# A graph kernel on one core: pairwise late statistics in the node stage, the degree roots moved ahead in the opening, and the filter kept in rows of 4 KB

## The reference

```python
deg = segment_sum([edge_weight, 1], [dst, loop]); r = rsqrt(deg)         # one root per node
agg = segment_sum((x @ W)[src_all] * (r[src_all]*w_all*r[dst_all])[:, None], dst_all)
x1  = layernorm(x + relu(agg + b))                                       # layer 1 with its residual
h   = softplus(rbf @ Wf1 + bf1) - log 2;  F = h @ Wf2 + bf2              # the filter, one row an edge
m   = F * (x1[dst] projected by Win_s, Win_v and the edge's direction Y) # messages
S, V = segment_sum(m * edge_weight, src) @ (W1, W2) with a softplus on S
out = layernorm(x1 + [S, V])                                             # layer 2 with its residual
```

## Time and profile before

| | |
|---|---|
| Time, median of 3 runs | 1192.75 us (1190.2 to 1195.69) |
| Profiled execution: its time, its span | 1193.07 us, 1191.3 us |
| Busy share of the span: PE, DVE, ACT, POOL | 84%, 70%, 59%, 55% |
| Mean granted TensorE clock | 0.902 of full speed |
| Moved by DMA | 289 MB, 243 GB/s on average |

### The profile page before, as it was taken

One profiled execution on the slowest core, in us unless ns is written; L12 is line 12 of the kernel. 1 busy time (PEld: TensorE's weight loads), 2 busy tenths in 40 slices (PEclk: granted clock), 3 DMA queues, 4 the chain that ended last, 5 costly groups with the idle time before them and its releaser, 6 DMA issues.

```text
span 1191.3 us, 23227 instructions
## 1 busy us (share of the span) xinstructions
PE 1000.9 (84%) x5088; PEld 790.9 (66%) x5088; DVE 835.9 (70%) x2538; ACT 701.7 (59%) x1632; POOL 660.3 (55%) x812
## 2 busy tenths in 40 slices
PE   7479998998838999999999399999999999634442
PEld 7458777776627888888888267777777777433332
DVE  8578876787606777787777366666666666368887
ACT  0068787777725666666666344444444444268887
POOL 3038888888745777777777546656566664400000
PEclk9999988999878999999999789999999999955555
DMA  9949999999986788878887669999999998589998
GB/s 356 418 156 235 245 228 229 247 253 227 220 170 207 265 276 279 277 277 278 278 277 263 235 161 211 194 202 195 205 194 208 195 205 177 69 256 347 351 351 287
DMA packets 175015, 289.00 MB, mean 243 GB/s; under 512 B 18514, under 2 KB 75750, under 8 KB 174966
## 3 DMA queue, kind: packets, MB, share of 16 engines
q1 hardware_dynamic: 120982, 176.23, 44.2%
q0 software_dynamic: 35840, 83.91, 36.7%
q10 hardware_dynamic: 18144, 28.32, 6.3%
HBM read 139.49 MB, written 148.90 MB: 242 GB/s over the span
## 4 chain that ended last, share of the span: by engine, by line
PE 30%; issue 17%; POOL 11%; DMA 5%; DVE 2%; ACT 2%; POOLq 2%; SPq 1%; ACTq 0%; DVEq 0%
PE bank L1084 6%; PE bank L1095 4%; POOL tiny L463 3%; PE bank L1093 3%; POOL tiny L466 3%; PE bank L1105 3%; PE bank L1107 3%; PE bank L1108 3%; DMA node_mem<-sum 3%; PE bank L1077 2%; PE bank L1085 1%; PE bank L1091 1%; PE bank L1057 1%; POOL tiny L470 1%; POOL tiny L468 1%
## 5 line engine op out<-in xcount | busy, mean ns | idle before, releaser
L500 POOL DMA_INDIRECT sum<-R_mem,l_sidx x80 | 128.0, 1600 | 126.1 <-ACT R_mem L625 74.3
L449 POOL DMA_INDIRECT sum<-R_mem,sidx_all x80 | 133.6, 1670 | 53.1 <-issue 29.1
L1057 PE MATMUL bank<-W0h,G_hi 128*128 128x512 f32 x320 | 134.0, 419 | 1.0 <-ACT G_lo L600 0.9
L1057 PE MATMUL bank<-W0l,G_hi 128*128 128x512 f32 x320 | 126.2, 394 | 0.0
L1057 PE MATMUL bank<-W0h,G_lo 128*128 128x512 f32 x320 | 126.2, 394 | 0.0
L611 ACT ACTIVATE node_mem<-node_mem,tiny 128x512 f32<-128x512 f32 x80 | 65.4, 818 | 91.7 <-POOL tiny L472 91.7
L476 POOL TENSOR_TENSOR G_lo<-node_mem,G_hi 128x512 fp32r<-128x512 f32 x80 | 104.4, 1305 | 17.8 <-ACT G_hi L607 17.8
L880 DVE SCALAR_TENSOR_TENSOR edge_mem<-edge_mem,Y,bank 128x128 f32<-128x128 f32 x240 | 72.5, 389 | 57.4 <-ACT edge_mem L639 57.4
L639 ACT COPY edge_mem<-bank 128x256 f32<-128x256 f32 x80 | 29.9, 373 | 134.3 <-PE bank L1095 134.3
L984 PE MATMUL bank<-G_hi,M_mem 128*128 128x512 f32 x200 | 88.5, 442 | 17.8 <-ACT R_mem L544 17.6
L492 POOL DMA_INDIRECT G_mem<-x_d,dst_i x80 | 79.5, 993 | 35.3 <-issue 23.2
(11 more groups left out here) (172 smaller groups left out, 2953.0 us busy)
## 6 DMA issues: line engine op xcount, KB each, us to landing
sum<-zeros ACTq DMA_DIRECT2D x42, 512.0 KB, 13.7
filt_d<-node_mem SPq DMA_DIRECT2D x40, 512.0 KB, 5.1
node_mem<-sum SPq DMA_DIRECT2D x80, 256.0 KB, 2.8
G_mem<-x SPq DMA_DIRECT2D x80, 256.0 KB, 2.8
x_d<-node_mem SPq DMA_DIRECT2D x80, 256.0 KB, 2.1
node_mem<-filt_d SPq DMA_DIRECT2D x80, 256.0 KB, 4.6
sum<-node_mem SPq DMA_DIRECT2D x80, 192.0 KB, 2.3
out<-G_mem SPq DMA_DIRECT2D x20, 512.0 KB, 4.2
```

The source lines that it names most:

```text
L449: pool.indirect_dma_start(sum0, bass.IndirectOffsetOnAxis(ap=sidx[:, t:t + 1], axis=0), R[t % 8][:, :], None, compute_op=ALU.add).then_inc ...
L500: pool.indirect_dma_start(sum1, bass.IndirectOffsetOnAxis(ap=l1_sidx[:, t:t + 1], axis=0), R3[t % 8][:, :], None, compute_op=ALU.add).then ...
L1057: ins = pe.matmul(bank[4 + a][:, :], zt[b][:, c * P:(c + 1) * P], w[:, c, :], start=(c == 0 and k == 0), stop=(c == 3 and k == 2))
```

## The change

**Node stage 0.** The sum is no longer split before the transposes. PE transposes it as float32 (four transposes), ACT casts the high part out of PSUM (`n_hi`), and DVE subtracts that from the same bank for the low part (`n_lo`). PE multiplies by W0 with the eight matmuls of the high part first. After the bias (`n_pre`), ACT takes the maximum with 0 (`n_rel`), POOL adds x (`n_sum`), and DVE takes statistics two steps later. The inverse root is made for two tiles at once, every second step, and the normalising lies at lag 9 where it lay at 6. The result has eight buffers, where it had four.

**Opening.** ACT issues 8 of the 42 DMAs of zeros and SP the other 34, behind the loads. The roots of the degrees are taken as soon as the degrees are there; Y and the scaled copies of W1 and W2 are made after edge stage 0. In the first two groups the comparisons of indices stand later on DVE, and the first sums earlier on PE and ACT. Gathers of a group share a semaphore.

**Filter.** `filt_d` has a row of 4 KB for two tiles, stored as it lies in its buffer, and is read two tiles at a time, 512 KB.

```diff
     x1_d = nc.dram_tensor("x1_d", (NP, D), F32, kind="Internal").ap()
-    filt_d = nc.dram_tensor("filt_d", (NP, D), F32, kind="Internal").ap()
+    filt_d = nc.dram_tensor("filt_d", (T2 * P, 2 * D), F32, kind="Internal").ap()
...
-        z_hi, z_lo = G_hi[:4], G_lo[:4]
+        zT_hi, zT_lo = G_hi[:4], G_lo[:4]
-        sl, res, W0_s = ([b[:, q * D:(q + 1) * D] for b in node_mem] for q in range(3))
+        sl, W0_s = ([b[:, q * D:(q + 1) * D] for b in node_mem] for q in (0, 2))
+        res = [b[:, q * D:(q + 1) * D] for q in (2, 3) for b in node_mem]
...
-        filt = [b[:, 0:512] for b in node_mem]
+        filt = [b[:, 0:1024] for b in node_mem]
...
+            for s in range(2):
+                sp_.dma_start(fT[s][:, :], rbf[:, s * Q:(s + 1) * Q]).then_inc(w_fT[s], 16)
+            sp_.wait_ge(s_zero, 1)
+            for j in range(NZ, 42):
+                sp_.dma_start(zero_rows(j), zeros[:, :]).then_inc(s_zero0, 16)
+
+
+            for s in range(2, T4 + 3):
                 if s < T4:
-                    if s >= 2:
-                        sp_.wait_ge(w_pre, s - 1)
+                    sp_.wait_ge(w_pre, s - 1)
                     sp_.dma_start(fT[s % 2][:, :], rbf[:, s * Q:(s + 1) * Q]).then_inc(w_fT[s % 2], 16)
                 if s >= 3:
                     for i in (2 * (s - 3), 2 * (s - 3) + 1):
                         sp_.wait_ge(w_eva, 4 * (i + 1))
-                        sp_.dma_start(pair_rows(filt_d, i, 0, D), wst[i % 4]).then_inc(w_st[i % 4], 16)
+                        sp_.dma_start(filt_d[i * P:(i + 1) * P, :], filt[i % 4]).then_inc(w_st[i % 4], 16)
 
...
 
             def nodes0(s, u):
-                a = u % 4
                 if live(s, 0):
-                    held(sp_, n_hi, s - 3)
-                    held(sp_, n_lo, s - 3)
+                    a = u % 4
+                    held(sp_, n_tr, s - 3)
...
-                    held(sp_, n_res, K_RES * (s - 7))
+                    held(sp_, n_sum, s - 7)
                     sp_.dma_start(xl[u], rows(x, s)).then_inc(n_xl[u], 16)
-                if live(s, 8):
-                    t = s - 8
+                if live(s, 12):
+                    t, a = s - 12, (u - 12) % 8
                     held(sp_, n_x1, t + 1)
                     sp_.dma_start(rows(x1_d, t), res[a]).then_inc(n_st[a], 16)
...
+            for g in range(T2):
+                if g >= 4:
+                    sp_.wait_ge(f_M, 2 * (g - 3))
+                sp_.dma_start(trow3[g % 4][:, :], src_row[:, g * 256:(g + 1) * 256].broadcast_to([P, 256])) \
+                   .then_inc(f_trow[g % 4], 16)
+                if g >= 4:
+                    sp_.wait_ge(f_m, 2 * K_PROD * (g - 3))
+                sp_.dma_start(filt[g % 4], filt_d[g * P:(g + 1) * P, :]).then_inc(f_filt[g % 4], 16)
...
-                    .then_inc(e_gather[k], 16)
+                    .then_inc(e_gather[k // 4], 16)
...
+                if live(s, 7) and u % 2 == 0:
...
+                    held(pool, n_mv, t + 2)
+                    st.mark(pool.tensor_scalar(w[:, 0, :], var, EPS, None, ALU.add))
+                    st.mark(pool.tensor_scalar(w[:, 7, :], mean, -1.0, None, ALU.mult))
+                    held(pool, n_rs, 2 * (g + 1))
+                    st.mark(pool.tensor_tensor(w[:, 3, :], w[:, 2, :], w[:, 2, :], ALU.mult))
+                    st.settle(pool)
+                    st.mark(pool.tensor_tensor(w[:, 4, :], w[:, 3, :], w[:, 0, :], ALU.mult))
...
+                    st.mark(pool.tensor_scalar(w[:, 3, :], w[:, 4, :], -0.5, 1.5, ALU.mult, ALU.add))
...
+                    st.mark(pool.tensor_tensor(w[:, 5, :], w[:, 3, :], w[:, 2, :], ALU.mult))
+                    st.settle(pool)
+                    st.mark(pool.tensor_tensor(w[:, 6, :], w[:, 7, :], w[:, 5, :], ALU.mult))
+                if live(s, 4):
+                    t, a = s - 4, (u - 4) % 8
+                    pool.wait_ge(n_rel, t + 1)
+                    pool.tensor_tensor(res[a], res[a], xl[a], ALU.add).then_inc(n_sum, 1)
...
+            for j in range(NZ):
+                act.dma_start(zero_rows(j), zeros[:, :]).then_inc(s_zero0, 16)
...
-                if live(s, 5):
-                    t, a = s - 5, (u - 5) % 4
-                    act.wait_ge(n_res, K_RES * (t + 1))
-                    act.activation(tiny[a][:, 1:2], mv[a][:, 1:2], ACT.Ln, bias=eps_c[:, :]).then_inc(n_rs, 1)
+                tail = live(s, 7) and u % 2 == 0
+                if tail:
+                    t, a = s - 8, u // 2
+                    g = t // 2 if isinstance(t, int) else (t - u) // 2 + a
+                    act.wait_ge(n_mv, t + 2)
+                    act.activation(tiny[a][:, 1, :], mv[a][:, :, 1], ACT.Ln, bias=eps_c[:, :]).then_inc(n_rs, 1)
                 if live(s, 2):
-                    b, t2 = u % 2, s - 2
-                    act.wait_ge(n_tr, s - 1)
-                    wait(act, n_mm, s - 3)
-                    act.copy(zT_hi[b][:, :], bank[b][:, :]).then_inc(n_zT, 1)
-                if live(s, 5):
-                    act.wait_ge(n_rs, 2 * t + 1)
-                    act.activation(tiny[a][:, 2:3], tiny[a][:, 1:2], ACT.Exp, scale=-0.5).then_inc(n_rs, 1)
-                if live(s, 2):
-                    act.copy(zT_lo[b][:, :], bank[2 + b][:, :]).then_inc(n_zT, 1)
+                    t2, b = s - 2, (u - 2) % 4
+                    act.wait_ge(n_tr, t2 + 1)
+                    wait(act, n_mm, t2 - 3)
+                    act.copy(zT_hi[b][:, :], bank[b][:, :]).then_inc(n_hi, 1)
...
+                if tail:
+                    act.wait_ge(n_rs, 2 * g + 1)
+                    act.activation(tiny[a][:, 2, :], tiny[a][:, 1, :], ACT.Exp, scale=-0.5).then_inc(n_rs, 1)
+                if live(s, 4):
+                    t4, c = s - 4, (u - 4) % 8
+                    act.wait_ge(n_pre, t4 + 1)
+                    act.activation(res[c], res[c], ACT.Relu).then_inc(n_rel, 1)
+                if live(s, 9):
+                    t8, c = s - 9, (u - 9) % 8
+                    k, b = c % 2, c // 2
+                    g8 = t8 // 2 if isinstance(t8, int) else (t8 - c) // 2 + b
+                    act.wait_ge(n_rstd, K_ROOT * (g8 + 1))
+                    act.activation(res[c], res[c], ACT.Identity, bias=tiny[b][:, 6, k:k + 1], scale=tiny[b][:, 5, k:k + 1]) \
                        .then_inc(n_x1, 1)
...
-            dve.wait_ge(s_sqrt, 2)
...
+            def inverse_root():
+                dve.wait_ge(s_sqrt, 1)
+
+                link(dve.reciprocal(dis[:, :], degs[:, :]))
+                link(dve.tensor_tensor(degt[:, :], degt[:, :], dis[:, :], ALU.mult))
+                link(dve.tensor_tensor(degt[:, :], degt[:, :], dis[:, :], ALU.mult))
+                link(dve.tensor_scalar(degt[:, :], degt[:, :], -0.5, 1.5, ALU.mult, ALU.add))
+                link(dve.tensor_tensor(dis[:, :], dis[:, :], degt[:, :], ALU.mult))
+                link(dve.tensor_tensor(dis[:, :], dis[:, :], deg[:, :], ALU.mult))
+                dve.sem_inc(s_dis, 1)
...
+                if s == 0:
+                    counts1()
+                    inverse_root()
+                if s >= 2:
+                    counts0()
+                    if s < T4:
+                        counts1()
                 if s >= 1:
                     if g >= 2:
                         dve.wait_ge(e_mm, 4 * (g - 1))
+                    dve.wait_ge(e_trow, g + 1)
...
+                    if s == 1:
+                        counts0()
+                        counts1()
...
+            dve.wait_ge(s_sqrt, 2)
+            link(dve.reciprocal(rn[:, :], rn[:, :]))
+            link(dve.scalar_tensor_tensor(Y[:, :, :], rij[:, :, :], Y1, rn[:, :].unsqueeze(2).broadcast_to([P, T, 3]),
+                                          ALU.mult, ALU.mult))
...
-                if live(s, 4):
                 if live(s, 0):
                     c = u % 4
                     dve.wait_ge(n_sl[c], 16 * (turn(s, c, 4) + 1))
                     dve.wait_ge(n_xl[u], 16 * (turn(s, u, 8) + 1))
                     dve.scalar_tensor_tensor(sl[c], xl[u], dis[:, bass.ds(s, 1)], sl[c], ALU.mult, ALU.add).then_inc(n_z, 1)
+                if live(s, 6):
+                    t, c, a = s - 6, (u - 6) % 4, (u - 6) % 8
+                    dve.wait_ge(n_sum, t + 1)
+                    dve.bn_stats(stat[c][:, :], res[a]).then_inc(n_bn, 1)
+                if live(s, 2):
+                    t, b = s - 2, (u - 2) % 4
+                    dve.wait_ge(n_hi, t + 1)
+                    wait(dve, n_mm, t - 3)
+                    dve.tensor_tensor(zT_lo[b][:, :], bank[b][:, :], zT_hi[b][:, :].bitcast(F32), ALU.subtract).then_inc(n_lo, 1)
+                if live(s, 6):
+                    t, a = s - 6, (u - 6) % 8
+                    k, b = a % 2, a // 2
+                    if k == 0:
+                        held(dve, n_x1, t - 6)
+                    held(dve, n_bn, t + 1)
+                    dve.bn_aggr(mv[b][:, k, :], stat[a % 4][:, :]).then_inc(n_mv, 1)
...
```

(57 more changed lines are left out.)

167 lines of the change are left out of this document (59 added, 108 removed).

## The result

The changed kernel takes 1149.33 us (median of 4 runs, 1146.42 to 1150.51), the kernel before 1192.33 in the same session: a ratio of 0.9633, 95% interval 0.9604 to 0.9662. The forecast was 1160, in a range from 1140 to 1184. The profiled execution took 1146.42, 46.65 less than the one profiled before.

A forecast was written before the change was run, and what follows sets the result against it. It took ACT's queue to delay the opening, DMA to bound edge stage 0, PE node stage 0 and edge stage 1. 1193.07 - 17.5 (opening) - 3 (filter) - 14 (node stage 0) + 1.5 (edge stage 1), less 0.3: 1160 us, range 1140 to 1184.

The forecast's parts named there:

- node stage 0's steps: Node stage 0: a tile every 3.55 us in place of 3.745, giving -15.6 us of the stage's -14.
- the opening: Start to first scatter: from 88.96 to 71.5 us, -17.5, bounds -20 and -13, carried through edge stage 0.
- the filter: Edge stage 0: half as many rows stored could shorten each group where the DMA is full; -3 us, bounds 0 and -10.
- The ready time of 63 to 68: Opening: when the first scatter's sums and indices would be ready, in us, ahead of the zeros' end near 71.5.
- Rival (C): Edge stage 0: swallows the opening's gain, its end doesn't move; 1177 us, chance 0.10.
- the stage is a chain of DMA: Edge stage 0: DMA-paced from the first scatter, share 0.99, a group every 13.29 us, so the whole stage shifts.
- The low ends give 3.44, the high ones 3.85. I take 3.55: Node stage 0: us per step from summing ACT's and DVE's durations and hand-overs around their waits.
- The ring: Node stage 0: a loop of waits between ACT and DVE sets the step at 3.55 us; PE at 3.25 idles.
- Rival (A): Node stage 0: ACT and DVE overlap more, the loop doesn't bind, PE decides at 3.3 us; 1140 us, chance 0.09.
- (B): Node stage 0: the loop over ACT and DVE is long, 3.85 us a tile; 1184 us, chance 0.12.
- (D): Node stage 0: PE loses its full clock, a tile takes 5.5 us; 1316 us, chance 0.04.
- The boundary: Last bias to first gather of edge stage 1: +2 us for the last tile leaving later, +1.5 for larger filter loads.

The follow-up runs named there:

- opening_old: The changed kernel with the opening of before (all 42 DMAs of zeros on ACT's queue, old order of the first groups): 1161.83 us, ratio 0.9762.
- node_alone: The kernel before with only the new node stage 0, opening and filter as before: 1160.09 us, ratio 0.973.
- no_store: The changed kernel with the filter's stores cut to 16 of 128 rows and every load reading the first block: 1151.65 us.
- the memsets: The changed kernel with two or four memsets added on POOL in each group of edge stage 0: 1163.32 us with two, 1174.17 with four.
- ring_broken: The changed kernel with DVE's bias placed ahead of its subtraction in node stage 0: 1139.68 us, ratio 0.9579; repeated, 1141.98 us, ratio 0.9574.
- ring_long: The changed kernel with DVE's scaled sum placed between its subtraction and its bias in node stage 0: 1199.54 us.
- pe_less: The changed kernel without the four matmuls of the low part in node stage 0, the waits kept: 1148.11 us.

## Why the prediction was right

**Right in the whole, one term too small by half.** The time lies in the range, and 10.7 us under the forecast. By the table, node stage 0's steps gave 18.6 more than I took, the opening 2.2 and the filter 2.9 less. So the total is nearer than its largest term, in part because the misses have opposite signs, which is luck.

**The opening: right in size, its last wait in one profile of two ways.** In the profile after, the zeros are late next, as forecast, at 73.7 where I had 71.5. That the last bytes trickle (57 GB/s from 70 to 75) is not in the estimate by bandwidth. The ready time of 63 to 68 was 69. In eight of the ten profiles with this opening it was about 74, behind degrees that came 5 us later, and POOL waited for that: the term is then -13.8 to -14.4, inside the bounds of -20 and -13, and the first group loses 2 to 5 us more. Rival (C), a gain swallowed in edge stage 0, is out as a whole by opening_old; that a part is swallowed, and how much, stays open after node_alone.

**The filter: the reason was wrong.** "Where the DMA is full, this could shorten each group" took the share of 0.99 as the bound, as did "the stage is a chain of DMA". no_store shows that the stage doesn't feel fewer bytes, and the memsets that it feels POOL's queue.

**Node stage 0: the mechanism right, its size wrong.** The step that failed is "The low ends give 3.44, the high ones 3.85. I take 3.55". The ring binds, as ring_broken, ring_long and pe_less show, but it is 3.38. I laid durations end to end: the subtraction with its aggregate is 0.70 from start to start and not 0.60 + 0.18, the maximum 0.54 where its row after says 0.63, the normalising 0.70 where its row says 0.80. An instruction here starts 0.08 to 0.10 us before the one ahead of it has ended. Nor did the ends that I wrote follow from the terms beside them: with the aggregate at 0.182 the low ones add up to 3.53, the high ones to over 4.2. The number that came is below both sums. DVE, ACT and POOL were busy for 2.65, 1.91 and 2.14 us a tile where I had 2.9, 2.1 and under 3.1; none of them sets the step. Besides, the steps of before were 3.767 by the biases, not 3.745. After, the first six steps run near PE's 3.20 until the ring holds them, which saves 1 us, and the last two, with less left to do, take 3.74 together, which saves 3: a mean of 3.334 over 79 steps, which makes the -34.2. What held the steps of before above PE's own 3.65 was not tested.

**Rival (A)** had the step's mean, 3.3, though not the time (its 1140 is 9 us under), and the wrong reason. PE at 99% looks like it. That PE is not what decides took pe_less to see. **(B)** is out. **(D)**: PE keeps clock 1.00 in node stage 0, with four transposes in every tile. The Trainium skill ("TensorE: Matmul & The Clock Gate", Part 4: PE-mode transpose) says that the full clock doesn't engage for such transposes; here they lie between matmuls, and the clock of 1.00 over 262 us shows no cost of it. Longer rows of transposes were not tried.

**The boundary** cost +4.7 for the 3.5 forecast: the last normalising starts 8.9 us behind the last bias (615.1 to 624.0), before 5.0 (666.9 to 671.9).

The experiments point to a better kernel than both: ring_broken, 1141.98 beside the changed kernel's 1156.95, and 1139.68 in its first runs. By its trace it is bound by PE in node stage 0 (253.00 of 253.00 us, the bias waiting for PE), and its edge stage 0 is as in the changed kernel; no run takes work off PE in it.

## What to carry to other kernels

In a stage with an order written by hand, follow one step around its waits and add up start-to-start spacings. If the sum comes near the busiest engine's need, two instructions in the other order can be worth a per cent, and a busy share of 99% on another engine doesn't exclude it. Before a DMA share near 1 is called the bound, ask which queue issues the transfers, and whether its instructions stand back to back.
